# Spreading the keys over the heads' rows: from one VectorE product and eight ScalarE copies to sixteen ScalarE copies, in an adaLN attention and mixture-of-experts kernel

## The reference, cut to what matters

```python
h = _layernorm(x, axis=-1) * (1 + ca) + sa
q, k, v = split_heads(h @ Wq), split_heads(h @ Wk), split_heads(h @ Wv)   # 16 heads of 16
logits = jnp.einsum('bhqd,bhkd->bhqk', q, ctx_k) * D_HEAD ** -0.5         # ctx: 4 sinks + window of 128
out = softmax(masked logits) @ ctx_v
x = x + ga * (out @ Wo)
h = _layernorm(x, axis=-1) * (1 + cb) + sb
x = x + gb * moe(h)          # shared expert + top 2 of 16 experts
```

## Time and profile before

| | us |
|---|---|
| median of three runs | 334.18 |
| lowest and highest run | 333.31 and 334.54 |
| profiled execution, first to last instruction (span) | 336.8 |
| busy in that span: TensorE matmul, VectorE, ScalarE, GpSimd | 269.9, 234.5, 164.9, 203.8 |

### The profile page before, as it was taken

How to read it: one execution, slowest core, us unless ns; L and a number is a source line. 1 busy time by engine, 2 the same in 40 slices (tenths; PEclk the granted TensorE clock), 3 DMA queues, 4 the chain that set the end, 5 groups by cost and what they waited for, 6 DMA issues and landing times.

```text
span 336.8 us, 5977 instructions
## 1 busy us (share of the span) xinstructions
PE 269.9 (80%) x1665; PEld 211.4 (63%) x1666; DVE 234.5 (70%) x900; ACT 164.9 (49%) x518; POOL 203.8 (61%) x255
## 2 busy tenths in 40 slices
PE   3897888888988988898966699999999989784000
PEld 3274457655856576656745699899998988673000
DVE  0477568998889888997887665644544777664980
ACT  3142372268345753368123356556565766554540
POOL 6604115847785587648655465566665678675971
PEclk9996999999999999999977799999999999999555
DMA  7939000124616529902265564455557778869793
GB/s 268 340 124 362 26 3 32 64 81 138 189 65 186 151 102 300 261 21 80 80 193 185 203 195 138 148 173 172 167 177 228 247 238 264 249 194 336 240 355 124
DMA packets 41436, 59.78 MB, mean 178 GB/s; under 512 B 5092, under 2 KB 29880, under 8 KB 41404
## 3 DMA queue, kind: packets, MB, share of 16 engines
q1 hardware_dynamic: 34312, 39.91, 39.8%
q0 software_dynamic: 6528, 17.90, 14.7%
q10 hardware_dynamic: 564, 1.59, 1.4%
HBM read 33.57 MB, written 25.80 MB: 176 GB/s over the span
## 4 chain that ended last, share of the span: by engine, by line
PE 52%; DVE 19%; DMA 9%; issue 8%; ACT 5%; POOL 3%; SPq 1%; POOLq 0%; DVEq 0%; ACTq 0%
PE bank L1253 14%; PE bank L914 7%; PE bank L1263 7%; PE bank L1110 6%; PE bank L1051 4%; DMA ys<-pt_win,row_i 3%; PE bank L928 3%; PE bank L1076 2%; PE bank L1130 2%; DMA p_win<-slots 2%; DMA ht<-in_L_attn_x_dram 2%; DVE h_sb L1396 2%; DMA w_gu<-ys 2%; PE bank L957 2%; DVE bank L1776 1%
## 5 line engine op out<-in xcount | busy, mean ns | idle before, releaser
L609 POOL DMA_INDIRECT slots<-h_sb,slot_i x64 | 63.6, 993 | 30.1 <-issue 15.3
L1253 PE MATMUL bank<-ht,v_wide 128*128 128x128 f32 x576 | 78.1, 280 | 3.2 <-issue 3.2
L1253 PEld LDWEIGHTS bank<-ht,v_wide 128*128 128x128 f32 x576 | 72.0, 196 | 3.5 <-issue 3.4
L664 POOL DMA_INDIRECT ys<-pt_win,row_i x40 | 38.8, 970 | 25.9 <-ACT pt_win L692 16.6
L692 ACT ACTIVATE ht<-bank 128x256 f32<-128x256 f32 x104 | 39.7, 382 | 17.9 <-PE bank L914 12.6
L1765 DVE TENSOR_TENSOR act_t<-bank,sg 128x128 f32<-128x128 f32 x72 | 20.9, 290 | 39.0 <-ACT sg L861 22.6
L1110 PE MATMUL bank<-w_route,ht 128*128 128x272 f32 x128 | 38.5, 425 | 7.6 <-ACT ht L692 5.6
L1263 PE MATMUL bank<-w_dn,act_t 128*128 x144 | 43.8, 386 | 0.8 <-issue 0.4
L664 POOL DMA_INDIRECT ys<-y_more,row_i x32 | 31.0, 968 | 18.8 <-ACT y_more L692 10.3
L914 PE MATMUL bank<-ident,p_win 128*128 128x128 f32 x198 | 36.2, 278 | 4.8 <-issue 2.9
L914 PEld LDWEIGHTS bank<-ident,p_win 128*128 128x128 f32 x198 | 26.6, 143 | 19.6 <-issue 9.3
(11 more groups left out here) (263 smaller groups left out, 516.6 us busy)
## 6 DMA issues: line engine op xcount, KB each, us to landing
p_win<-slots SPq DMA_DIRECT2D x67, 129.0 KB
slots<-pads SPq DMA_DIRECT2D x28, 129.0 KB
xs<-in_L_attn_x_dram SPq DMA_DIRECT2D x3, 1024.0 KB
wmod_sb<-ys SPq DMA_DIRECT2D x12, 256.0 KB
w_gu<-ys SPq DMA_DIRECT2D x10, 256.0 KB, 2.8
mod_bc<-mod_rows_out SPq DMA_DIRECT2D x4, 512.0 KB, 5.3
w_dn<-in_L_ffn_w_down_dram SPq DMA_DIRECT2D x1, 2048.0 KB
h_sb<-ys SPq DMA_DIRECT2D x8, 256.0 KB
```

Source lines behind the costliest of these rows:

```text
L609: pool.indirect_dma_start(out=slots, out_offset=bass.IndirectOffsetOnAxis(ap=slot_i[:, k, j:j + 1], axis=0), in_=h_sb[:, j, :], in_offset= ...
L664: pool.indirect_dma_start(out=ys, out_offset=bass.IndirectOffsetOnAxis(ap=row_i[:, col:col + 1], axis=0), in_=y_sb[y], in_offset=None).the ...
L1253: last = mm(bank[2 + k % 2][:, half * P:(half + 1) * P], w_now[:, k, c, half * M:(half + 1) * M], ht[:, k, c, :], start=(c == 0), stop=(c ...
```

## The change

The first half of the keys is no longer spread by VectorE but by ScalarE, in eight instructions in two sets of four heads, each set with a count of `at_ks`. The second half is now written to columns 256 to 383 of bank 6, the bank of the values, and is spread by ScalarE after `at_v`. `at_q` is counted by the queries' last matmul. The logits of heads 0 to 3 wait for the first set and the queries, those of heads 4 to 7 for the second set, and those of heads 8 to 11 for the second half.

```diff
+            def first_keys(b, heads):
+
+                act.wait_ge(S["at_k"], b + 1)
+                for i in heads:
+                    last = act.activation(kt_bd[:, 0, i, :], bank[5][:, 0:P], ACT.Copy, scale=own_rows[:, i:i + 1])
+                    if i % 4 == 3:
+                        last.then_inc(S["at_ks"], 1)
+
             def second_keys(b, heads):
 
+                act.wait_ge(S["at_v"], b + 1)
                 for i in heads:
-                    last = act.activation(kt_bd[:, 1, i, :], bank[4][:, 2 * P:3 * P], ACT.Copy,
+                    last = act.activation(kt_bd[:, 1, i, :], bank[6][:, 2 * P:3 * P], ACT.Copy,
                                           scale=own_rows[:, i:i + 1])
...
             act.wait_ge(S["const"], N_CONST)
+            first_keys(0, range(CH))
             queries(0)
             second_keys(0, range(CH))
...
                 if b > 0:
                     tanh(b, 0)
+                    first_keys(b, range(0, 4))
                     queries(b)
-                    second_keys(b, range(0, 3))
                     act_copy(b, 0)
                 h_copy(b, 0)
...
                 else:
-                    second_keys(b, range(3, CH))
+                    first_keys(b, range(4, CH))
+                    second_keys(b, range(0, CH))
                     own_values(b)
...
                 for w, c, o, s in ((wk_sb, 0, bank[5][:, 0:P], "at_k"), (wq_sb, 0, bank[4][:, 0:P], None),
-                                   (wq_sb, 1, bank[4][:, P:2 * P], None), (wk_sb, 1, bank[4][:, 2 * P:3 * P], "at_q")):
+                                   (wq_sb, 1, bank[4][:, P:2 * P], "at_q"), (wk_sb, 1, bank[6][:, 2 * P:3 * P], None)):
...
                 if g == 0:
 
-                    pe.wait_ge(S["at_ks"], b + 1)
+                    pe.wait_ge(S["at_ks"], b * 2 + 1)
+                    pe.wait_ge(S["at_qs"], b * 2 + 1)
+                elif g == 1:
+                    pe.wait_ge(S["at_ks"], b * 2 + 2)
+                elif g == 2:
                     pe.wait_ge(S["at_qs"], b * 2 + 2)
...
-            def at_keys(b):
-
-                dve.wait_ge(S["at_k"], b + 1)
-                v.tensor_tensor(kt_bd[:, 0, :, :], bank[5][:, 0:P].unsqueeze(1).to_broadcast([P, CH, P]),
-                                own_rows[:].unsqueeze(2).to_broadcast([P, CH, P]), ALU.mult).then_inc(S["at_ks"], 1)
...
-            at_keys(0)
-
             dve.wait_ge(S["setup_ps"], SMALL_V)
...
                 if not first:
-                    at_keys(b)
                     chosen(b * GPB - 1)
```

## The result

The changed kernel took 335.38 us (median of ten runs, 333.74 to 337.46), the kernel before 333.14 us beside it (median of ten). The ratio on record is 1.0092, with a 95% interval of 1.0061 to 1.0122: slower, by 2.0 to 4.1 us. It is the record's own comparison of the executions and not the quotient of the two medians, which differ by 2.2 us (1.0067). The forecast was 335.8 us, inside a range of 333.4 to 337.3. All ratios are of executions at the usual speed; the one that was profiled first for `tanh_before_second` was not one of them (690.6 us, its commonest matmul 538 ns long and not 279, though its record names no lower clock), and its trace is not read.

What follows compares the result with a forecast made beforehand. No engine was full; the bound was the chain of waits, where VectorE's activation(b, 1) waits for ScalarE's tanh(b, 1). Three batches 0.54 us later each, batch 0 nothing, gave +1.62: 334.2 to 335.8 us, range 333.4 to 337.3.

Steps and rivals of the forecast that it cites:

- rival A: ScalarE's block is still longer, from a late count or spreads spaced up to 0.29 us: 336.4, up to 337.3 us; chance 0.25.
- Rival B: VectorE and h_copy set the end, so earlier gate_up(b, 1) wins 2.85 us: 331.3 us; chance 0.13.
- The edits priced at nothing: Spreads in the hole, the at_v wait, earlier gate_up(b, 1) and batch 0 were each costed at 0.
- The four spreads in the hole: First four spreads run in ScalarE's 2.49 us idle time after tanh(b, 0): cost nothing, 1.0 us without that cover.
- The wait for `at_v`: In second_keys on ScalarE: the values' matmuls are over before the second spreads' turn at 106.5, so cost nothing.
- The earlier `gate_up(b, 1)`: On TensorE it starts 0.95 us earlier, at 105.67, but its three followers do not profit: costed at nothing.
- The cover: Batch 0: ScalarE is done at about 24.4, GpSimd takes its results at 25.17; cost 0, without this cover 0.7 us.
- The sum: Batches 1 to 3 lose 3 x 0.54 = 1.62 us, batch 0 nothing; median from 334.2 to 335.8 us.
- an oddity: On ScalarE, qt starts 1.02 us after the recorded end of the last key group, though it waits only for its count.
- the 0.95 us gain of the forecast: Counting at_q on the queries' last matmul brings h_copy(b, 0) on ScalarE forward from 106.15 to 105.20.
- the forecast 0.54: Delay per batch of VectorE's activation(b, 1), at about 109.93 instead of 109.39; 0.74 us with a late count.
- No slack to swallow that: After activation(b, 1), slot_i, four scatters, wsd_gated and down(b, 3) are all 0.54 us late, with no slack found.

Runs made afterwards that it cites:

- tanh_before_second: Changed kernel with the eight spreads of the keys' second half moved right behind tanh(b, 1): 330.86 us, ratio 0.9958; measured again 331.04 us, 0.9958.
- The dose experiment: Changed kernel with four more spreads per batch in batches 1 to 3, behind h_copy(b, 0) (338.88 us, 1.0191) or in ScalarE's hole (335.07 us, 1.0094).
- first_half_on_vector: Kernel before with only the other edits (bank 6, at_v wait, queries' count, split waits); the keys' first half stays on VectorE: 331.89 us, ratio 0.9982.
- before_again: Kernel before, unchanged, first of three further profiles; the three profiled executions took 330.78, 332.57 and 333.68 us.
- after_again: Changed kernel measured once more, no edit: 335.09 us, ratio 1.0085 [1.0056, 1.0113].
- count_on_fourth: Changed kernel with the at_q count put back on the last of the four matmul groups: 334.41 us, ratio 1.0081.
- before_fourth: Kernel before, unchanged, last of three further profiles; ratio 1 as the reference.
- four_more_late: Changed kernel with four more spreads per batch in batches 1 to 3, right behind h_copy(b, 0): 338.88 us, ratio 1.0191.
- before_third: Kernel before, unchanged, second of three further profiles; ratio 1 as the reference.
- four_more_in_hole: Changed kernel with four more spreads per batch in batches 1 to 3, placed where ScalarE idles, before the first four: 335.07 us, ratio 1.0094.
- tanh_first_load_later: Changed kernel with the eight second-half spreads behind tanh(b, 1) and the last w_up load issued two tiles later: 329.82 us, ratio 0.9922.

## Why the prediction was right, and what of it was not

**The mechanism was right.** The forecast said that VectorE's saving would be worth nothing because `activation(b, 1)` waits for the tanh, and that the tanh would be later because twelve spreads stand before it. It put the tanh 4.33 us behind `h_copy(b, 0)`; it came 4.34 us behind (106.28 to 110.62). The spacing stayed at 0.25 us, so the wider spacing of rival A was not seen, nor the 0.29 that the page estimate of the Trainium skill (ScalarE: Activation LUTs, section What ACT_TABLE_LOAD costs) had given. VectorE idled for over 1 us (2.13), TensorE for 1.12 us before the logits of heads 8 to 11. The dose experiment shows the price per instruction at this place, `tanh_before_second` shows that the place is the cause, and the same dose in the hole shows the cover. Rival B named its own condition, eight or fewer of the twelve spreads before the tanh; `tanh_before_second` met it, with four, and was faster: 0.9958. With all twelve in place B did not happen.

**The edits priced at nothing** were worth nothing. The four spreads in the hole: shown, even eight fit there. The wait for `at_v`, the bank and the split waits: `first_half_on_vector` shows no loss. The earlier `gate_up(b, 1)`: it was earlier only against the first profile (3.41 us after `tanh(b, 0)` against 4.43), while in `before_again` it starts at 3.44. In batch 0 ScalarE ended its centres at 25.11 in the profile after, and GpSimd, waiting for its data from memory, took them at 26.05; that batch's matmuls of queries and keys start 0.67 us later in this execution than in the earlier trace rows's, upstream of every edit in the batch. The cover held, with 0.94 us to spare. From the start of these matmuls to `tanh(b, 0)` of batch 1 it is 48.28 us after and 48.23 before, so batch 0 cost nothing. The expectation of `after_again` charged 0.7 us to a stretch at the lower clock there. That stretch is 6.8 us long in both profiles and ends 1.6 us later after (35.7 against 34.2), and no loss goes with it.

**The term that was mis-sized is the reference of the per-batch loss.** The sum took `tanh(b, 1)` at 108.73 from the profile of before, saw that `qt` there started 1.02 us after its matmuls' end, called it an oddity, and went on: the changed count should bring `h_copy(b, 0)` forward by 0.95 us. Three more profiles of before show that the lag belonged to that one execution. In the others `ht` stands at 2.98 us, where the change leaves it too (2.97), and `count_on_fourth` shows that moving the count buys nothing. So the 0.95 us gain of the forecast does not exist in an ordinary execution, and the tanh is 1.74 us later than in an ordinary execution (7.31 against 5.57) and not 0.80. That it cost less than 1.74 has its own reason. With a prompt count VectorE reached L1403 at 7.15 us after `tanh(b, 0)`, busy until then with its own work; after the change it starts at 7.78. The loss is the difference of these, 0.63 us a batch, and `slot_i` moves by 0.64 (10.01 to 10.65), batch 1 by 0.63 (35.65 to 36.28). Two errors nearly cancelled: a gain that was not there, and a slack of 1.24 us on the other side of the hand-over that the first profile did not show. Against the first profile the delay was 0.58 us at L1403, close to the forecast 0.54, and 0.38 at `slot_i`.

**Luck in the number.** The forecast counted from a median of 334.18 us, of three runs; ten runs have 333.14. The change itself was forecast at +1.6 us and measured at +2.2 by the medians and about +3 by the ratio. That 335.8 lies within 0.5 us of 335.38 is so in part because the starting point was 1.0 us too high and the change too small.

**"No slack to swallow that" held for two batches of three, and probably for the third.** Batches 1 and 2 kept the delay. Batch 3 seems to keep only 0.27 to 0.33 us of it (37.60 against 37.27 to 37.33). But in all four profiles of before the stretch at the lower clock lies in batch 3, and in the changed kernel it does not. `first_half_on_vector`, which has no such stretch in batch 3 either, is 0.81 us shorter than the changed kernel in batch 1 and 0.80 us in batch 3. So it is likely that batch 3 keeps the whole delay too, and that the kernel before loses about half as much there to the lower clock. No run was made to test this.

**A cost that the sum did not have** is the landing of scatters behind the load of `w_up` in batch 2. It makes that batch longer than batch 1 by 0.3 us in some profiles and by some 0.85 in others (only `before_fourth`, with its long batch 1, fits neither). The larger value is in both profiles of the changed kernel and in `four_more_late`, but also in `before_third`, and `count_on_fourth` and `four_more_in_hole`, with the same spreads, have the smaller one. So it is shown that the load costs this time and that a later load removes it; it is not shown that the change brings it about.

**The sum, redone.** For batches 1 to 3, four profiles with the twelve spreads in place (after, after_again, count_on_fourth, four_more_in_hole) have a mean sum of 110.73 us and four of before 109.43: +1.3 us; against the three with a prompt count (109.19) it is +1.5. The forecast had +1.6. The measured loss is 2.0 to 4.1 us by the first interval and 1.9 to 3.8 by the second. So about half of it is placed. Batch 0 gives nothing, so the rest would have to lie after the last tanh. The stretch from the last tanh to the end takes 154.2, 154.3 and 154.9 us in the three prompt profiles of before and 157.7, 156.7, 154.8 and 156.0 in the four above (mean 156.3, or +1.8). In the three the clock is at the upper level there until the last 26 us or so. In the four it drops for 3.4 us once, in one of them twice. The first profile of before, which drops twice there, takes 160.4. So the stretch at the lower clock is a candidate for the open part: in the prompt profiles of before it falls into batch 3, where it costs about 0.35 us (1.65 or 1.67 against 1.30 to 1.34), and in the four into the routed experts' tiles. It is not shown that the change moves it: `tanh_first_load_later` drops there too, takes 155.7 and is the fastest of all.

## What to carry to other kernels

Price a moved instruction by its place in the queue and not by its engine's load. In the changed kernel a spread of 0.25 us costs its whole time in front of the tanh that another engine waits for, and nothing that is seen in a hole; the version with eight of them behind that tanh beats both kernels. When work goes from the fuller engine to the emptier one, find the hand-over between the two and work out on both sides when each arrives. The emptier engine may come later by as much as the fuller one was behind it (here 1.24 us), and what goes beyond that is loss (1.74 us later cost 0.63 us). And if one row of a single profile looks odd, as a count that comes 1 us late does, take a second profile before building a term on it; if there is only one, work out the sum with and without the oddity on both sides of the difference. Before comparing a stage between two profiles, look at the granted clock of that stage in both.

## What was not expected of the hardware

The count of a finished group of matmuls reached ScalarE 1.02 us after the group's recorded end in batches 1 to 3 of one execution of the kernel before, and 0.03 us after it in three others of the same program. In the other kernels' profiles, where an instruction of ScalarE in batch 2 waits directly for such a count, it starts 0.03 to 0.04 us after the group's recorded end. What makes an execution of the one kind or the other stays open; the three prompt ones ran on two chips, and on which the first ran is not on record.

One load with elements of 0.5 KB took 6.2 us from issue to landing, and in the kernel after, of the four scatters issued behind it, no count arrived before its own last one, though the first had been issued 5.3 us earlier. VectorE waited for 1.88 us; with the load elsewhere it waited for 0.54.

An instruction of VectorE that took 0.48 us took 0.95 us beside a product of GpSimd that started 0.06 us ahead of it, in all three batches of three profiles (0.88 to 0.95).

A stretch of 3.4 us at granted clock 0.50 fell into batch 3 in all four profiles of before and behind the last tanh in the two of the changed kernel. `gate_up`'s four matmuls took 2.02 us in it in place of 1.08.
